# Attention pipeline: order of the second rows' transposes, of the query projection and of the row statistics

## What is computed

```python
# x: (32, 256, 256), ctx: (32, 120, 256), 16 heads of 16
xn = layernorm(x)
q, k, v = split(xn @ Wq), split(ctx @ Wk), split(ctx @ Wv)
attn = softmax(q @ k.T * HEAD_DIM ** -0.5)        # row maximum, exp, row sum
x = x + (merge(attn @ v) @ Wp + bp)
xn2 = layernorm(x)                                # normalised again for the router
logits = (xn2 / rms(xn2) * norm_weight) @ router_weight.T + router_bias
...                                               # top-k of tokens per expert, two matmul layers, scatter-add
```

## Time and profile before

| what | value |
|---|---|
| median of 3 runs | 966.09 us (965.4 to 966.34) |
| the profiled execution: its own time, its span | 965.09 us, 963.4 us |
| PE busy, PEld busy | 855.3 us (89%), 732.4 us (76%) |
| DVE, ACT, POOL busy | 741.0, 510.5, 593.4 us |
| attention | the first 19 of 40 slices (24 us each) |
| granted TensorE clock in the attention's steady part (60 to 430 us) | full (1.00, the 2.4 GHz level) |

### The profile page before, as it was taken

How to read it: one execution, slowest core, us unless ns; L and a number is a source line. 1 busy time by engine, 2 the same in 40 slices (tenths; PEclk the granted TensorE clock), 3 DMA queues, 4 the chain that set the end, 5 groups by cost and what they waited for, 6 DMA issues and landing times. The chain is left out here.

```text
span 963.4 us, 21098 instructions
## 1 busy us (share of the span) xinstructions
PE 855.3 (89%) x6159; PEld 732.4 (76%) x6159; DVE 741.0 (77%) x1662; ACT 510.5 (53%) x929; POOL 593.4 (62%) x567
## 2 busy tenths in 40 slices
PE   8799999999999999999811159999999999999995
PEld 7678888788878887887611147989999999999985
DVE  4588888888888888887599766888777777777642
ACT  3456655665566556655366127465555555555541
POOL 4157666766676667665552356688877766775344
PEclk9899999999999999999855569999999999999998
DMA  5456665666566666654241033466665666665333
GB/s 174 153 196 202 217 215 201 206 214 222 198 201 218 211 201 207 219 200 150 86 146 44 14 103 122 157 176 174 167 166 158 162 160 163 166 173 147 93 71 44
DMA packets 129510, 156.51 MB, mean 162 GB/s; under 512 B 22449, under 2 KB 104625, under 8 KB 129345
## 3 DMA queue, kind: packets, MB, share of 16 engines
q1 hardware_dynamic: 104064, 113.05, 36.3%
q0 software_dynamic: 15616, 25.70, 12.5%
q10 hardware_dynamic: 9792, 17.31, 4.9%
HBM read 74.93 MB, written 26.28 MB: 105 GB/s over the span
## 5 line engine op out<-in xcount | busy, mean ns | idle before, releaser
L599 DVE TENSOR_REDUCE NM<-bank 128x4 f32<-128x480 f32 x256 | 155.5, 650 | 61.1 <-PE bank L761 61.0
L424 ACT ACTIVATE PT<-bank 120x512 f32<-120x512 f32 x256 | 142.5, 603 | 36.1 <-PE bank L786 34.9
L348 POOL TENSOR_SCALAR XN<-X,mv,rstd 128x256 f32<-128x256 f32 x124 | 150.5, 1222 | 14.1 <-POOL rstd L343 13.3
L1691 PE MATMUL bank<-W2H,HH 128*128 128x256 f32 x512 | 144.7, 283 | 2.0 <-issue 2.0
L1693 PE MATMUL bank<-W2H,HL 128*128 128x256 f32 x512 | 143.6, 280 | 0.0
L1692 PE MATMUL bank<-W2L,HH 128*128 128x256 f32 x512 | 143.5, 280 | 0.0
L1147 POOL DMA_INDIRECT out_dram<-C,IO x60 | 111.9, 1865 | 50.6 <-issue 31.3
L1417 DVE TENSOR_TENSOR HL<-hf,HH 128x512 fp32r<-128x512 f32 x128 | 87.3, 690 | 50.6 <-ACT HH L1572 49.9
L786 PE MATMUL bank<-QX,KX 128*120 128x256 f32 x512 | 110.6, 309 | 8.8 <-DMA QX<-NMT 5.2
L557 DVE RECIPROCAL RR<-RC 128x256 f32<-128x256 f32 x64 | 111.4, 1742 | 5.4 <-DMA RC<-PVS 5.3
L1567 ACT ACTIVATE hf<-bank,B 128x512 f32<-128x512 f32 x128 | 87.8, 686 | 41.4 <-PE bank L1693 35.5
(11 more groups left out here) (198 smaller groups left out, 1909.8 us busy)
## 6 DMA issues: line engine op xcount, KB each, us to landing
QX<-QH ACTq DMA_DIRECT2D x64, 256.0 KB
W<-w1T_dram SPq DMA_DIRECT2D x16, 1024.0 KB, 5.6
W<-w2T_dram SPq DMA_DIRECT2D x16, 1024.0 KB
X<-x_dram SPq DMA_DIRECT2D x32, 256.0 KB, 3.1
QX<-QL SPq DMA_DIRECT2D x32, 256.0 KB
XB<-x_dram SPq DMA_DIRECT2D x32, 256.0 KB, 2.9
RC<-PVS SPq DMA_DIRECT2D x64, 128.0 KB, 2.1
OC<-PVS SPq DMA_DIRECT2D x64, 128.0 KB, 2.2
```

Of the source, the lines that this page charges most:

```text
L348: ins = pool.tensor_scalar(dst[:, t, :], src[:, t, :], mv[:, t, 0:1], rstd[:, t:t + 1], ALU.subtract, ALU.mult)
L424: act.activation(PT[u][0:M, HE * k:HE * (k + 1), :], score_bank(b, k // 2)[k % 2][0:M, :], ACT.Exp, scale=SCALE) \
L599: dve.tensor_reduce(NM[u][:, t, :].rearrange("p (f n e) -> p n e f", n=HN, e=HE)[:, n, :, :], smax_bank[q % 2][:, 0:4 * M].rearrange("p (e ...
L1691: pe.matmul(o, wh, xh, start=first, stop=False)
```

## The change

Three edits, all of order:

```diff
@@ DVE step
             for q in range(4):
                 row_max(q)
-            rows()
+            early = known(i) and 2 * i + c < 0
+            if early:
+                rows()
             if known(i) and 2 * i + c == -3:
                 first_rows()
             for q in range(4, NQ):
                 row_max(q)
             low_queries()
+            if not early:
+                rows()
@@ PE queries
-            def queries():
+            def queries(halves):
...
-                    for e in range(HE):
+                    for e in halves:
...
-                    ins.then_inc(q_done, 1)
+                    if HE - 1 in halves:
+                        ins.then_inc(q_done, 1)
@@ PE step
             max_scores(1)
+            rows2()
             scores(4)
-            rows2()
             scores(5)
...
             if first != -1:
-                queries()
+                queries((0,))
             max_scores(6)
+            if first != -1:
+                queries((1,))
             max_scores(7)
             if first == -1:
-                queries()
+                queries((0, 1))
```

## The result

The changed kernel takes 968.9 us (median of 14 runs, 967.23 to 970.5), the kernel before 965.36 us (14 runs, 961.33 to 966.82). The ratio is 1.0042, with a 95% interval of 1.003 to 1.0054: slower, by 3.5 us, which is the loss that was forecast; the forecast time of 969.6 us started from 966.09 us, the median of three runs. Of all runs in this document one, of edits 1 and 2 without edit 3, took 1014.5 us at a granted clock of 0.81 in place of 0.94; it is left out of the medians.

What follows compares the result with a forecast made beforehand. A two-step loop over DVE, POOL, SP and QL's DMA to PE was taken to bind: 27.59 + 0.73 - 0.25 - 0.13 = 27.94 us per pair, ten pairs 3.5 us, hence 969.6 us; range 964.8 to 972.2.

Steps and rivals of the forecast that it cites:

- Edit 1: Second rows' transposes moved ahead of scores(4) in the attention, filling PE's wait for an exp; gain 0.13 us per step.
- Edit 2: Queries in halves around row-maximum group 7; up to 0.35 us off the gap at L774, q_done about 0.22 later.
- Edit 3: Statistics of X moved behind QL; after the mark (group 8's loads end) X1 at + 4.12, xn_table 0.73 us later.
- rival (a): Another loop binds, DVE/PE (13.6 us per step) or ACT/PE (13.96, turn step); time stays, 966 us; chance 0.28.
- The loop that was named: Two-step loop through DVE, POOL, SP and QL's DMA to PE's max_scores(0); grows from 27.59 to 27.94 us per pair.
- Rival (b): Only PE's own waits count, up to 0.35 us at L774 and 0.13 per step; 961 us; chance 0.10.
- Rival (c): QL and neighbours collide with other transfers as SP's issues bunch; 0.4 us more per turn step, 974 us; chance 0.07.

Runs made afterwards that it cites:

- edits 1 and 2 without edit 3: The changed kernel with the statistics of X back between row maxima 4 and 5; 960.8 us (median of six runs), ratio 0.9956 to the kernel before.
- edit 2 alone: The kernel before with only the queries split in two halves around row-maximum group 7; 965.2 us, ratio 1.0003.
- split in c = 0 only: Changed kernel, statistics in their old place, queries split only in loop steps c = 0, whose end no branch follows; 958.32 us, ratio 0.9922 to the kernel before.
- edit 3 alone: The kernel before with only the statistics of X moved behind QL, PE's order as before; 976.03 us, ratio 1.0119.

## Why the prediction was right, and where it was not

**The direction, the size and the place.** The forecast was 3.5 us in the loop of steps, 0.35 us per pair. The pair grew by 0.28 us. Between the transposes of the maxima nearest to the loop's two ends, at 108.10 and 412.12 us before and at 108.53 and 415.78 us after, 22 steps take 304.02 and 307.25 us: 3.2 us.

```profile
108.53 0.10 PEld L779 LDWEIGHTS bank<-ident,NM 128*16 128x16 f32 x2 [0.41 <-issue]
...
415.78 0.10 PEld L779 LDWEIGHTS bank<-ident,NM 128*16 128x16 f32 x2 [0.41 <-issue]
```

**Edit 1, 0.13 us per step.** Alone it gave 0.17 (27.59 less 27.25, halved). The reading that the exps take over from the wait was right: all 0.32 would have been 8 us.

**Edit 2.** Row maximum 8 came at + 0.24, as worked out, and the gap ahead of L774 went to 0.41 us. q_done's 0.22 us showed in full: edit 2 alone made the turn step 14.10 us against 13.87. The run with the split in c = 0 only fits the way it takes through ACT: its pair is 27.12, where 27.17 was expected.

**Edit 3, the chain from the mark.** X1 at + 4.12 was + 4.23 in the plain step; xn_table at + 10.3 was + 10.43. That the statistics have no cover in their new place, which is the term with the largest share, was right. POOL's ve of X1 stood directly behind XN in the plain step, but waited 0.45 us for DVE in the turn step, where X1 was at + 4.83. DVE's idle time moved as forecast: 1.00 us before row maximum 5 and 0.43 before 8.

**The failed step is in rival (a), and with it in the choice between loops.** DVE's chain was priced at 13.6 us per step for both kinds of step. In the plain step it is 13.62. In the turn step DVE has a turn of its own to pay, which the trace of before does not show; as I read it, the branch was taken there while the last row maxima and QL ran. The statistics, moved to the very end of the step, took that cover away: 13.62 + 0.6 = 14.2 us, where 13.6 was written and 14.25 measured. I had asked what covers the statistics, and not what they uncover.

**The loop that was named is not the one that sets the pair.** It was worked out to 27.94 us. Two of its terms were mis-sized: QL's issue to the loads, taken as 2.78, is 2.52 us in the changed kernel and again with late statistics in c = 0 only, both times behind a wait (the 2.78 and 2.77 before stood behind none), and from `max_scores(0)` to the mark it is 7.31, where 7.10 was taken, because of DVE. With the measured 2.52 its sum is 27.7, and the run with late statistics in c = 0 only, where it does bind, has a pair of 27.58.

So that loop, as measured, would have left the pair as it was (27.59), which is rival (a), and the time with it: the two experiments that keep edit 3 in part but not the 0.59 us on DVE (statistics ahead of QL, and late in c = 0 only) came out at 965.04 and 965.46 us. The direction and the size of the forecast came true by luck: a loop priced 0.3 us too long was named, and another, priced 0.6 us too short in the turn step, gave the loss. The mechanism as first named would have pointed to SP as the place to mend. No run issued QL sooner and left DVE as it was. The run of edit 3 alone comes nearest: PE does not wait for QL there, and the loss is there all the same.

The Trainium skill (DMA: Bandwidth & Descriptors, section Anatomy of one DMA) gives its 2.0 us plus bytes at 436 GB/s for DMAs that GpSimd issues, while SP issues this one. The 2.60 us worked out from it, an estimate, are nearer to the 2.52 us from QL's issue to PE's load than my 2.78. The landing itself stands in no row.

**Rival (b)** had 13.6 us for both steps: the plain step has it, the turn step with 14.25 does not. **Rival (c)**, transfers in each other's way, would have made QL later than taken; at 2.52 us it was sooner.

**What stays open.** What DVE does in the 0.59 us of a turn stands in no row. And the profiled executions differ before the loop of steps too. The stretches from 39 to 54 us (columns: stretch, its length, busy us of PE, PEld, DVE, ACT and POOL with counts, granted clock, DMA share, GB/s) have, in the kernel before and then in the changed one,

```profile
39.00:54.00 15.00, 13.13 (x111) 10.07 (x113) 10.95 (x19) 8.17 (x16) 7.12 (x8) 1.00 0.54 176
```

```profile
39.00:54.00 15.00, 13.17 (x101) 10.17 (x94) 10.83 (x19) 7.97 (x16) 5.86 (x6) 0.89 0.52 164
```

The granted clock was 0.89 against 1.00, that is, for part of this stretch TensorE ran at 1.2 in place of 2.4 GHz. The same 0.89 stands in the runs with edits 1 and 2 and with the split in c = 0 only, which are faster than before, so it does not make the difference; whether the edits cause it was not tried.

## What to carry to other kernels

Before an operation is moved to the end of a loop's body, ask what it then stands in front of. Here a pair of operations with a wait between them, moved directly ahead of the loop's branch, brought out 0.59 us per turn that had been hidden; that the wait is what does it is the reading that fits all runs, not shown by one of its own. Put such a pair (BN_STATS, wait, BN_AGGR) where something long still runs between its end and the branch, or where the engine waits for another anyway; moved from there onto the path, it costs what it takes. And where several engines' loops lie within 1% of each other, work each of them out for each kind of step, since a loop body of two steps can have two different bounds, and an edit that pays in one may be kept out of the other.

## What was not expected of the hardware

A turn of a loop cost nothing on DVE where row maximum 8 and QL ran ahead of it without a wait for PE (QL to reciprocal 0.60 us in either kind of step before), and 0.59 us where the statistics with their wait stood last. With QL between the statistics and the branch, 0.12 us of it was left, and with row maximum 8 waiting for PE, in edits 1 and 2, 0.13. On SP the same turn shows as 1.31 us from RC(1) to QL, against 0.75 in a plain step, and on ACT as 1.23 us from its first DMA of QH to the PVS copy, against 0.73 (both in the kernel before).
